# Perceiver block on one core: folding the query weights before the other early transfers are in

## The reference

```python
x = x + xattn(layernorm(x), ctx, seg_id)     # 16 heads, latent keys, rotary part, window of 8 keys behind seg_id
x = x + attn(layernorm(x))                   # 16 heads, the mask multiplies the scores
x = x + ffn(layernorm(x))                    # 8 experts, top 2 of a sigmoid router, and 2 shared experts
```

```python
kv_c = ctx @ W_kvc;  q_c = q @ W_dq
q_nope = q_c @ W_uq; q_rope = rope(q_c @ W_qr)
k_nope = kv_c @ W_uk; k_rope = rope(kv_c @ W_kr); v = kv_c @ W_uv
scores = (q_nope . k_nope + q_rope . k_rope) * scale, only keys in [seg_id - 8, seg_id]
out = softmax(scores) v @ W_o
```

## Time and profile before

| | |
|---|---|
| three runs | 557.5, 560.95, 562.01 us |
| the profiled execution, its own time | 562.37 us |
| its span | 560.6 us |
| PE busy | 532.9 us (95%), 4468 matmuls |
| DVE busy | 268.3 us (48%) |
| ACT busy | 162.4 us (29%) |
| POOL busy | 58.8 us (10%) |
| mean granted clock of TensorE | 0.982 of full speed |

### The profile page before, as it was taken

One profiled execution on the slowest core, in us unless ns is written; L12 is line 12 of the kernel. 1 busy time (PEld: TensorE's weight loads), 2 busy tenths in 40 slices (PEclk: granted clock), 3 DMA queues, 4 the chain that ended last, 5 costly groups with the idle time before them and its releaser, 6 DMA issues.

```text
span 560.6 us, 11604 instructions
## 1 busy us (share of the span) xinstructions
PE 532.9 (95%) x4468; PEld 390.0 (70%) x4468; DVE 268.3 (48%) x573; ACT 162.4 (29%) x306; POOL 58.8 (10%) x70
## 2 busy tenths in 40 slices
PE   7979999999999989998699999999999999999996
PEld 6667787787888878886477777555555555556774
DVE  3547767767776357888444222122222222222244
ACT  1244434534444315444221111122211221121111
POOL 2000000000000013122102341000000000000450
PEclk9699999999999999999889999999999999999999
DMA  9600000000594076000252115468888778761231
GB/s 302 258 0 20 20 1 19 19 1 18 177 396 196 2 307 261 2 0 1 69 214 76 49 56 212 157 215 289 306 280 284 270 289 311 268 215 63 66 104 66
DMA packets 24457, 82.06 MB, mean 146 GB/s; under 512 B 2881, under 2 KB 16513, under 8 KB 20322
## 3 DMA queue, kind: packets, MB, share of 16 engines
q1 hardware_dynamic: 21536, 75.93, 37.2%
q0 software_dynamic: 1536, 4.20, 2.3%
q10 hardware_dynamic: 1346, 1.38, 0.8%
HBM read 73.11 MB, written 8.39 MB: 145 GB/s over the span
## 4 chain that ended last, share of the span: by engine, by line
PE 86%; DVE 5%; issue 4%; DMA 2%; ACT 1%; POOL 0%; SPq 0%; DVEq 0%; POOLq 0%
PE ps L1626 16%; PE ps L1585 13%; PE ps L1192 11%; PE ps L1653 8%; PE ps L1613 6%; PE ps L1226 5%; PE ps L1245 5%; PE ps L1270 5%; PE ps L1258 3%; PE ps L1463 3%; DMA w_routed<-in_w_qr 2%; PE ps L1241 1%; PE ps L1218 1%; PE ps L1511 1%; DVE w_routed L588 1%
## 5 line engine op out<-in xcount | busy, mean ns | idle before, releaser
L1626 PE MATMUL ps<-w_routed,xnT 128*64 x320 | 93.8, 436 | 0.6 <-issue 0.6
L1585 PE MATMUL ps<-w_shared,xT_all 128*128 128x384 f32 (+1 forms) x256 | 76.6, 444 | 0.0
L1160 ACT COPY hidT<-ps 128x384 f32<-128x384 f32 x36 | 17.2, 479 | 181.0 <-PE ps L1192 176.1
L1626 PEld LDWEIGHTS ps<-w_routed,xnT 128*64 128x64 f32 x320 | 42.0, 137 | 37.4 <-issue 26.1
L1585 PEld LDWEIGHTS ps<-w_shared,xT_all 128*128 128x128 f32 x256 | 48.2, 195 | 18.0 <-issue 2.8
L889 DVE COPY hidT<-ps 128x256 f32<-128x256 f32 x36 | 15.3, 424 | 92.9 <-PE ps L1192 90.2
L1192 PE MATMUL ps<-consts_a,w_routed 128*128 128x128 f32 x400 | 51.7, 275 | 6.2 <-ACT w_routed L1012 2.9
L1192 PEld LDWEIGHTS ps<-consts_a,w_routed 128*128 128x128 f32 x400 | 44.5, 141 | 13.5 <-issue 4.6
L1653 PE MATMUL ps<-w_routed,hidT 128*64 x200 | 47.4, 384 | 0.0
L1626 PE MATMUL ps<-w_shared,xnT 128*64 128x384 f32 (+1 forms) x160 | 46.9, 436 | 0.0
L1626 PE MATMUL ps<-x_up,xnT 128*64 128x384 f32 (+1 forms) x160 | 46.9, 436 | 0.0
(11 more groups left out here) (175 smaller groups left out, 879.4 us busy)
## 6 DMA issues: line engine op xcount, KB each, us to landing
w_routed<-in_w_routed SPq DMA_DIRECT2D x8, 1920.0 KB, 14.1
x_up<-in_w_routed SPq DMA_DIRECT2D x10, 1280.0 KB, 5.7
w_shared<-in_w_routed SPq DMA_DIRECT2D x10, 1280.0 KB, 6.0
b_down<-in_w_routed SPq DMA_DIRECT2D x10, 640.0 KB, 5.5
w_shared<-in_w_routed SPq DMA_DIRECT2D x10, 640.0 KB, 4.9
w_shared<-in_w_shared SPq DMA_DIRECT2D x1, 3840.0 KB, 12.1
w_shared<-in_w_uvo SPq DMA_DIRECT2D x1, 2560.0 KB, 15.5
x_slots<-sil SPq DMA_DIRECT2D x16, 160.0 KB, 2.2
```

The lines of the kernel that those rows point to most:

```text
L1160: act.copy(hidT[:, 0:3, :], ps[:, 4, 0:CA].rearrange("p (c t) -> p c t", t=P)).then_inc(hT_a, 1)
L1585: last = pe.matmul(ps[:, b, 0:hi - lo], xT_all[:, i, k, :], w[:, at:at + hi - lo], start=k == 0, stop=k == KT - 1)
L1626: last = pe.matmul(ps[rows, b, 0:hi - lo], xnT[:, k, rows], w, start=k == 0, stop=k == KT - 1)
```

## The change

The query fold gets a semaphore of its own (`wu_in`, raised by the transfer of w_uqk) and comes right after the zeros, of which there are 9 instead of 12. The key fold follows behind a wait for the other three transfers and writes into bank 6 instead of bank 0. The wait for `const_in` moves behind it, and the wait for the key fold's copy moves behind `qc(0)`. ScalarE copies the query fold first and then the key fold. On DVE `front_k(0)` and `front_q(0)` come between the maximum and the minimum of the far search.

```diff
-WARM_UP = 12
+WARM_UP = 9
...
-            sp.dma_start(w_shared[:].rearrange("p e n -> p (e n)")[:, 0:H * (QC + KVC)], dram["w_uqk"]).then_inc(wk_in, 16)
+            sp.dma_start(w_shared[:].rearrange("p e n -> p (e n)")[:, 0:H * (QC + KVC)], dram["w_uqk"]).then_inc(wu_in, 16)
...
             link(dve.tensor_reduce(far[:, 0:1], seg_row, AX.X, ALU.max))
+            front_k(0, link)
+            front_q(0)
             link(dve.tensor_reduce(far[:, 1:2], seg_row, AX.X, ALU.min))
             link(dve.tensor_scalar(far[:, 2:3], far[:, 0:1], float(P - 1), None, ALU.is_gt))
             link(dve.tensor_scalar(far[:, 3:4], far[:, 1:2], 0.0, None, ALU.is_lt))
             dve.tensor_tensor(far_i[:], far[:, 2:3], far[:, 3:4], ALU.add).then_inc(far_ready, 1)
 
-            front_k(0, link)
-            front_q(0)
             front_qt(0)
...
-            act.wait_ge(absorb_k_ps, 1)
-            act.copy(w_k[:, :, KVC:], ps[:, 0, 0:KT * R].rearrange("p (k r) -> p k r", r=R)).then_inc(absorb_k, 1)
             act.wait_ge(absorb_q_ps, 1)
             act.copy(w_q[:, 0].rearrange("p h c -> p (h c)"), ps[0:QC, 2:4, :].rearrange("p b n -> p (b n)")).then_inc(absorb_q, 1)
+            act.wait_ge(absorb_k_ps, 1)
+            act.copy(w_k[:, :, KVC:], ps[:, 6, 0:KT * R].rearrange("p (k r) -> p k r", r=R)).then_inc(absorb_k, 1)
...
             keep_warm(WARM_UP)
-            pe.wait_ge(wk_in, 16 * 4)
-            pe.wait_ge(const_in, 16 * 2)
-            for k in range(KT):
-                last = pe.matmul(ps[:, 0, k * R:(k + 1) * R], w_kvcT[:, k * P:(k + 1) * P], w_kr[:], start=True, stop=True)
-            last.then_inc(absorb_k_ps, 1)
+            pe.wait_ge(wu_in, 16)
             for h in range(H):
                 last = pe.matmul(ps[0:QC, 2 + h // 8, (h % 8) * KVC:(h % 8 + 1) * KVC], w_uq[:, h, :], w_uk[:, h, :],
                                  start=True, stop=True)
             last.then_inc(absorb_q_ps, 1)
-            pe.wait_ge(absorb_k, 1)
+            pe.wait_ge(wk_in, 16 * 3)
+            for k in range(KT):
+                last = pe.matmul(ps[:, 6, k * R:(k + 1) * R], w_kvcT[:, k * P:(k + 1) * P], w_kr[:], start=True, stop=True)
+            last.then_inc(absorb_k_ps, 1)
+            pe.wait_ge(const_in, 16 * 2)
             xT(0)
             qc(0)
+            pe.wait_ge(absorb_k, 1)
             pe.wait_ge(absorb_q, 1)
             kv(0)
```

More of the change, by code:

```diff
@@ L266, in build @@
         b_dn_in = [sem(f"b_dn_in{q}") for q in range(2)]
-        names = """const_in x0_in x_in wk_in wv_in wo_in aw_in ctx_in win_ready dve_step pool_step
+        names = """wu_in const_in x0_in x_in wk_in wv_in wo_in aw_in ctx_in win_ready dve_step pool_step
             absorb_q_ps absorb_q absorb_k_ps absorb_k absorb_m_ps absorb_m
@@ L274, in build @@
         S = {n: sem(n) for n in names}
-        (const_in, x0_in, x_in, wk_in, wv_in, wo_in, aw_in, ctx_in, win_ready, dve_step, pool_step,
+        (wu_in, const_in, x0_in, x_in, wk_in, wv_in, wo_in, aw_in, ctx_in, win_ready, dve_step, pool_step,
          absorb_q_ps, absorb_q, absorb_k_ps, absorb_k, absorb_m_ps, absorb_m,
```

## The result

The changed kernel took 557.32 us (median of 20 executions, 555.15 to 561.68), the kernel before 560.91 us (20 executions, 557.5 to 563.34). The ratio is 0.9932, with a 95% interval of 0.9913 to 0.9951, so 3.8 us or 0.7% less; the two medians are 3.6 apart. That is inside the range, 1.0 above the forecast of 556.3, and under the 1% that the prediction named as the least that can be told from no change.

The account below looks back on a forecast made before the run. A serial prologue delays a body that PE bounds; zeros, folds and y reordered gain 5.3 us, capped at 5.5 by w_uvo. That gives 557.1 from the profiled execution or 555.7 from the median; forecast 556.3, range 553.8 to 560.2.

Parts of the forecast that it names:

- Zeros and query fold: Prologue on PE: 9 zeros end at 7.4, query fold follows without a wait to 10.1, key fold at 11.3.
- The low clock moved over to xT, qc and kv: Prologue after the key fold: clock falls at 12.3 as before, all three keep old durations, kv ends at 15.9.
- y: Four y matmuls after kv: 4.21 us, range 3.5 to 6.9, ending at 20.1 (19.4 to 22.8).
- Value fold: After y and w_uvo (19.8): starts 20.1, takes 3.63, ends 23.7, 5.3 us early; the transfer caps the gain at 5.5.
- DVE: Rotations and far search: moving them buys nothing; copy of transposed queries starts 0.5 late, scores at 27.3.
- The gain at the end: Whole kernel: 5.3 us gained, giving 557.1 from the profiled execution, 555.7 from the median; 556.3 predicted between them.
- rival (b): Old kernel's prologue: executions without the clock's fall never paid; 5 us of gain vanish, 560 if the median is such; chance 0.15.
- it moves as a whole: Everything after the prologue: hangs on the same engines' semaphores, no later DMA in the chain, so the 5.3 us carry through.
- if the body gives the time back: Attention body after the prologue: a sign that would show the prediction wrong; no size given.
- (a): Prologue: clock stays low through y, value fold 22.8 to 26.4, gain 2.6, 558.4 from the median; chance 0.15.
- (c): Prologue: clock low until after the value fold, which ends at 30.0; scores at 34.6, slower at 563.0; chance 0.05.
- (d): Later in the span: clock episodes fall elsewhere, adding or taking 1 to 2 us, with luck 553.5; chance 0.13.

Follow-up runs that it names:

- x later with zeros: Changed kernel, transfer of x beyond tile 1 behind ScalarE's query fold copy, plus 3 zero matmuls between query fold and key fold: 554.85 us, ratio 0.986.
- zeros in the gap: Changed kernel with 3 more zero matmuls between the query fold and the wait for w_qr: 557.45 us, ratio 0.9933.
- x later: Changed kernel with the transfer of x beyond tile 1 issued behind ScalarE's copy of the query fold: 556.04 us, ratio 0.9894.

## Why the prediction was right

**Zeros and query fold.** Predicted: zeros to 7.4, fold 7.4 to 10.1, key fold at 11.3. Measured: the fold began at 6.8, and ended at 9.75; the key fold came at 10.87. The slow opening passes ended earlier in this execution, so the fold did wait, 0.28 us for w_uqk, where the prediction had no wait; and w_qr was in 0.4 earlier.

**The low clock moved over to xT, qc and kv.** Predicted: they keep their durations, `kv` ends at 15.9. Measured: 0.63, 1.17 and 1.71, end at 15.55.

**y.** Predicted 4.21, with 3.5 to 6.9 open. Measured 4.79 in this profile, 4.0 with the far search in its old place and 3.44 where the clock stayed up. Value fold predicted at 20.1, measured 20.34, done at 23.97 in place of 23.7. w_uvo landed at 4.28 + 15.5 = 19.8, unmoved by tile 1's context, which SP issued at 15.75. Those two transfers took 7.7 and 7.9 us to land, against 2.3 and 3.4 before. So the later transfers waited and the earlier wasn't slowed. "DMA: Bandwidth & Descriptors" in the Trainium skill, section "Two DMAs through the same engine are not ordered", says that the descriptors in one queue of one engine start in order, and this agrees with it. The prediction had that no row shows two such transfers side by side; the trace before does have a pair, consts_b (234 KB), issued at 4.84 behind w_uvo, which landed only at 20.6, behind it.

**DVE.** Predicted: line 588 starts 0.5 late, at 25.6, and the scores at 27.3 don't wait for it; the move buys nothing. Measured 25.64, 27.54, and a ratio with the move undone that is the same.

**The gain at the end.** 5.3 predicted in the prologue, 5.0 measured in the profile, 3.8 over 20 executions of each. Two things can make the difference; both show in profiles, and how much each weighs over the 20 executions does not.

The first is rival (b), executions of the kernel before in which the clock hardly falls: 558.4 at a mean clock of 0.994, and by its time the run of 557.5. No profile of one exists, so it isn't shown that the fall which they lack is the prologue's. The run with 18 zeros stands in for them, the old order without that fall: its scores start at 29.22, or 28.3 without the 0.9 by which its zeros overran, against 26.8 to 27.5 with the new order, so 0.8 to 1.5 us of the gain remain there. I let that case keep 1 us at most, which is about right, but by a wrong sum: from a query fold done at 14.7 I had y end at 19 to 20 and w_uvo cap the old order too. The run with 18 zeros takes 9.8 us from the start of the key fold to the end of y (12.20 to 22.02), which from 11.28 is 21.1. So y and not w_uvo limits the old order, and that is why something remains.

The second is a term that the sum had at nothing: "it moves as a whole". The clock can fall in tile 0's body once the prologue is shorter, and then 1.4 to 1.7 us are given back. That was my own sign of being wrong, "if the body gives the time back". The profile of the changed kernel doesn't have it (233.4 in both), and the one that differs from it only in the far search does: 5.3 us won by the scores, 3.6 left at line 495.

The 556.3 was 1.0 too low. It lay between a sum from one profiled execution, in which the clock did fall for 10 us, and one from the median, and both took the whole 5.3. That the choice between them came out so near is in part luck: executions of one kernel scatter by 6 us.

**Rivals (a) and (c)**, a clock that stays low through y or the value fold, did not show in any profile of the new order: it rose at 18 or so at the latest, or never fell in the prologue. **(d)** is real in size: the turn to the third block and what follows it made 2.2 us between the two profiles. I take that for chance and not the change, since the profile of x later with zeros has the long turn as well (10.8 us between GpSimd's two instructions) and the run with 18 zeros in the old order the short one (9.65).

## What to carry to other kernels

Where PE waits for a first transfer, look at which work's own data are already there, and give it its own semaphore; but look first at the granted clock behind the wait, since here 3.3 of 5.0 us came back with a few more idle matmuls in the old order. When a serial prologue gets shorter, the next limit is the next transfer: here, wherever y ended in time, it held the scores at 26.8 to 27.2 until a transfer that nobody needed yet was issued later. Compare many executions when the clock falls in some and not in others: one pair of profiles showed 7.2 us of a difference of 3.8. And follow a gain past the place where it was made: here 1.4 to 1.7 us of it were lost again in the next stage in six profiles.

## What the runs showed of the hardware that was not expected

The same idle stretch was followed by a fall in one execution and by none in another. In tile 0's body PE idles for 2.9 us in each of the eleven profiles where nothing fills this wait. In six the granted clock fell to 0.50 within the last 0.7 us of it or the first microsecond behind it (at 30.6 to 34.4); in five (the kernel before, with 12 zeros and with 9, the change, 12 zeros in the new order, zeros in the gap) it stayed at 1.00. In the prologue 1.1 us of idle was followed by a fall (the changed kernel, at 11.3), and 1.3 us was not (x later). At the turn to the third block it fell in all 13 profiles, once or twice.

The opening of the kernel doesn't show in the granted clock at all: it reads 1.00 from 1 to 6.8 us, while the same 18 passes of zeros took 5.79 us in one profile (the change) and 7.07 in another (x later with zeros in the gap). "TensorE: Matmul & The Clock Gate" in the Trainium skill, Part 1, has it that activity releases a clock that is low by default and that the point varies from run to run; the lengths of the zeros agree with that.

For a pause of PE like the 2.65 us above, the profile names no cause.
